# Cross attention of a decoder in groups of 4, 4, 4, 2 and 2 batches, and an expert layer with weights loaded a layer earlier and its sums in parts

## The reference

```python
# part 5: the weighted key-value recurrence of layer 1; reads ctx by channels only
# part 6: the experts of layer 1 (16 experts, 4 for each token, at most 128 tokens an expert)
scores = softmax(x @ gate_w.T)
topk_w, topk_i = top_k(scores, 4);  topk_w = topk_w / topk_w.sum(-1)
xg   = x[tokens of expert e]                                   # gathered rows
mid  = silu(xg @ w_gate[e]) * (xg @ w_up[e])                   # 176 wide
y[tokens of expert e] += (mid @ w_down[e]) * weight
shared = (silu(x @ sw_gate) * (x @ sw_up)) @ sw_down           # 352 wide
out  = y + shared
# part 8: the cross attention of layer 2, ctx as keys and values
Q      = x @ W_q.T
scores = coef * einsum('bsd,bnd->bsn', Q, ctx)                 # 128 x 128 for each batch
thr    = the 54th largest score of each row
att    = softmax(where(scores < thr, -inf, scores))
out    = einsum('bsn,bnd->bsd', att, ctx) @ W_o.T
```

## Time and profile before

| | us |
|---|---|
| three runs | 2928.51, 2930.05, 2932.92 (median 2930.05) |
| the profiled execution | 2934.89 |
| its span | 2933.1 |
| from the span's start: recurrence begins | 1411.1 |
| experts begin | 1517.7 |
| layer 2 attention begins | 1675.1 |
| cross attention begins | 2151.4 |
| layer 2 feed-forward begins | 2279.5 |

### The profile page before, as it was taken

How to read it: one execution, slowest core, us unless ns; L and a number is a source line. 1 busy time by engine, 2 the same in 40 slices (tenths; PEclk the granted TensorE clock), 3 DMA queues, 4 the chain that set the end, 5 groups by cost and what they waited for, 6 DMA issues and landing times. The chain is left out here.

```text
span 2933.1 us, 45191 instructions
## 1 busy us (share of the span) xinstructions
PE 2248.4 (77%) x18630; PEld 1725.2 (59%) x18679; DVE 1900.4 (65%) x3121; ACT 1283.9 (44%) x1627; POOL 353.7 (12%) x161
## 2 busy tenths in 40 slices
PE   7975278999999999997138789999953457877643
PEld 4654146777777767777124579999933224554422
DVE  5765677778887788875882434334437785773676
ACT  4642155666666666664422133333321343443144
POOL 0000012222232222320115000000000011000000
PEclk9987689999999999998569899999986679997867
DMA  3000121122121221222125400000000000000000
GB/s 131 1 1 12 23 64 49 54 75 55 49 54 56 73 55 50 53 60 72 61 82 146 166 23 0 0 0 0 0 8 1 30 0 24 2 1 15 1 29 29
DMA packets 159610, 117.72 MB, mean 40 GB/s; under 512 B 116176, under 2 KB 146000, under 8 KB 153680
## 3 DMA queue, kind: packets, MB, share of 16 engines
q1 hardware_dynamic: 156368, 110.99, 12.3%
q0 software_dynamic: 3072, 4.33, 0.9%
HBM read 97.64 MB, written 17.64 MB: 39 GB/s over the span
## 5 line engine op out<-in xcount | busy, mean ns | idle before, releaser
L1447 DVE SCALAR_TENSOR_TENSOR ctx_chan<-l1a_raw,l1a_cw,ctx_chan 128x1024 f32<-128x1024 f32 x192 | 230.8, 1275 | 19.5 <-ACT ctx_chan L1298 18.5
L1060 PE MATMUL banks<-x_chan,l1a_wp 128*128 128x512 f32 x512 | 230.6, 604 | 5.0 <-DMA l1a_wp<-in_l1a_wp_dram 5.0
L1024 POOL TENSOR_TENSOR l1a_sq<-ctx_chan 128x1024 f32<-128x1024 f32 x16 | 152.3, 9517 | 356.7 <-ACT ctx_chan L1302 356.7
L1060 PEld LDWEIGHTS banks<-x_chan,l1a_wp 128*128 128x128 f32 x512 | 98.1, 194 | 116.9 <-issue 110.8
L2475 PE MATMUL banks<-x_chan,l2a_wq 128*128 (+1 forms) x1024 | 124.2, 282 | 9.5 <-ACT l2a_ready L2378 4.9
L2475 PEld LDWEIGHTS banks<-x_chan,l2a_wq 128*128 128x128 f32 x1024 | 122.6, 198 | 11.4 <-issue 5.6
L1097 PE MATMUL banks<-l1a_wo,l1a_oT 128*128 128x256 f32 x512 | 121.8, 387 | 0.0
L1045 POOL TENSOR_TENSOR l1a_al<-l1a_aT,l1a_outer 128x1024 f32<-128x1024 f32 x32 | 74.8, 2359 | 327.2 <-DVE l1a_aT L1507 327.2
L2496 PE MATMUL banks<-l2a_wo,l2a_oT 128*128 128x256 f32 x512 | 113.2, 379 | 1.2 <-ACT l2a_oT L2402 1.2
L96 PE MATMUL banks<-ident,x_tok 128*128 128x128 f32 x288 | 56.8, 360 | 74.5 <-DVE x_tok L134 58.5
L1068 PE MATMUL banks<-l1a_wz,x_chan 128*128 128x256 f32 x512 | 113.7, 380 | 0.0
(11 more groups left out here) (604 smaller groups left out, 5908.2 us busy)
## 6 DMA issues: line engine op xcount, KB each, us to landing
ctx_tok<-l1a_rows_mem SPq DMA_DIRECT2D x16, 1024.0 KB, 6.6
l1a_sq<-l1a_norm_mem SPq DMA_DIRECT2D x16, 1024.0 KB, 4.5
ctx_tok<-in_ctx_dram SPq DMA_DIRECT2D x3, 2048.0 KB, 12.4
ctx_chan<-in_ctxT_dram SPq DMA_DIRECT2D x3, 2048.0 KB, 15.8
l1f_wgu<-in_l1f_wgu_dram SPq DMA_DIRECT2D x4, 1408.0 KB, 10.7
moe_sums<-l1x_zero SPq DMA_DIRECT2D x2, 2176.0 KB, 11.0
l1a_wp<-in_l1a_wp_dram SPq DMA_DIRECT2D x8, 512.0 KB, 3.3
l1f_wgu<-moe_sums SPq DMA_DIRECT2D x8, 512.0 KB, 8.1
```

What stands on the lines that cost most here:

```text
L1024: P.tensor_tensor(sq[:, 0, :], conv[:, 0, :], conv[:, 0, :], ALU.mult).then_inc(s["k_squared"], 1)
L1060: mm = MM(ps[:, 2 * (u % 2) + q, :], wp[:, c, u * 128:(u + 1) * 128], g.xT[:, c, t0:t0 + 512], start=c == 0, stop=c == 1)
L1447: V.scalar_tensor_tensor(t, raw[:, u, :, j:j + S], cw[:, c, j:j + 1], t, ALU.mult, ALU.add).then_inc(s["conv_done" if step == 2 else "conv ...
```

## The change

**Weights.** The last step of layer 1 attention no longer loads `ctx` into `g.mem`. The recurrence loads all of wd0 (2 MB, one transfer) there. The expert part then loads gate, up and wd1 of batches 0 and 1 at once, the routing weights behind them, and batches 2 and 3 once the eighth gather has landed.

**Experts.** `shared_in(3)`, its silu and its product are moved ahead of the experts. The sums are added quad by quad between the products of the shared chunks, and the normalising goes in parts of 8, 4 and 4 tiles.

**Cross attention.** The four quads of queries and scores follow each other, ACT moves and scales the scores, and DVE selects in groups of 4, 4, 4, 2, 2 batches. ACT takes the negated maximum as the exponential's bias. DVE makes mask, product and sum in one instruction for each batch, ACT divides before the transposes, PE adds x with a matmul by the identity, ACT moves the sum into x, and DVE takes the statistics of group n - 1 behind the selection of group n. Fourteen tiles are normalised while the last group is attended. wq and wo are laid out by partitions in DRAM.

```diff
@@ layer1_delta, SP
-            sp.dma_start(g.mem[:].rearrange("p b d -> p (b d)"), d["ctx"]).then_inc(s["restored"], 16)
             sp.dma_start(g.memT[:].rearrange("p c t -> p (c t)"), d["ctxT"]).then_inc(s["restored"], 16)
-            sp.wait_ge(s["restored"], 32)
+            sp.wait_ge(s["restored"], 16)
@@ layer1_wkv, SP
+            sp.dma_start(g.mem[:].rearrange("p b d -> p (b d)"), g.dram["l1f_wd0"]).then_inc(s["wd_loaded"], 16)
...
@@ layer1_moe, SP
             for n in range(4):
+                if n == 2:
+                    sp.wait_ge(fetched[RING - 1], 16)
                 sp.dma_start(wgu[:, e].rearrange("p e c h n -> p (e c h n)"), d["l1f_wgu"][n]).then_inc(w_loaded[n], 16)
-                sp.dma_start(wd0[:, e, :].rearrange("p e n -> p (e n)"), d["l1f_wd0"][n]).then_inc(w_loaded[n], 16)
                 sp.dma_start(wd1[:, e, :].rearrange("p e n -> p (e n)"), d["l1f_wd1"][n]).then_inc(w_loaded[n], 16)
-                if n == 0:
+                if n == 1:
                     sp.wait_ge(s["weights_made"], 1)
@@ layer1_moe, PE (ACT and DVE likewise: shared_silu(3), shared_mid(3))
             shared_in(2)
+            shared_in(3)
...
             def turn_mid(e):
+                if e == 0:
+                    pe.wait_ge(s["sh_mid"], 4)
...
-                for k in range(3):
-                    shared_in(3 * q + k)
+                for n in range(max(3 * q, 4), 3 * q + 3):
+                    shared_in(n)
@@ layer1_moe, DVE
-            for q in range(1, QUADS):
-                for k in range(3):
-                    shared_mid(3 * q + k)
-                if q < QUADS - 1:
-                    add_shared(q - 1)
-                if q == 2:
-                    v.wait_ge(s["sh_done"], 4)
-                    add_routed(0)
-                    add_routed(1)
+            shared_mid(4)
+            shared_mid(5)
+            add_shared(0)
+            v.wait_ge(s["sh_done"], 2)
+            shared_mid(6)
+            add_routed(0)
+            shared_mid(7)
+            shared_mid(8)
+            add_shared(1)
+            v.wait_ge(s["sh_done"], 4)
+            shared_mid(9)
+            add_routed(1)
+            shared_mid(10)
             add_routed(2)
-            add_shared(2)
+            shared_mid(11)
             add_routed(3)
             stats(0, 8, (s["chain"], count[0]))
-            stats(8, 12, (s["sh_done"], 6))
+            add_shared(2)
+            stats(8, EARLY, (s["sh_done"], 6))
             moments(0, EARLY)
+            normalise(0, 8, 1)
             add_shared(3)
...
@@ layer2_cross, PE, for each group (t0, t1) of GROUPS = ((0, 4), (4, 8), (8, 12), (12, 14), (14, 16))
+                pe.wait_ge(s["normed"], n + 1)
+                for i in range(t0, t1):
+                    mm = nc.tensor.transpose(ps[:, turned, (i - t0) * 128:(i - t0 + 1) * 128], probs[:, i, :], g.ident[:])
...
+                        nc.tensor.matmul(now, g.ident[:], g.x[:, i, :], start=True, stop=False)
+                        for c in range(DC):
+                            mm = nc.tensor.matmul(now, oT[:, i, c, :], wo[:, c, :], start=False, stop=c == 1)
@@ layer2_cross, ACT
+            for n in range(len(GROUPS)):
+                normed(n)
+                if n < len(GROUPS) - 1:
+                    exps(n + 1)
+                else:
+                    A(g.scratch[:], g.ones[:, 0:1], ACT.Sqrt)
+                    act.wait_ge(s["ln_var"], 1)
+                    A(g.rstd[:, 0:EARLY], g.rstd[:, 0:EARLY], ACT.Sqrt).then_inc(s["ln_sqrt"], 1)
+                attended(n)
@@ layer2_cross, DVE
+                v.wait_ge(s["exped"], n + 1)
+                for t in range(t0, t1):
...
+                    ins = V.scalar_tensor_tensor(probs[:, t, :], sc[:, t, :], best[:, t, at:at + 1], probs[:, t, :], ALU.is_ge, ALU.mult, accum_out=rsum[:, t:t + 1])
+                ins.then_inc(s["kept"], 1)
+                v.wait_ge(s["kept"], n + 1)
+                V.reciprocal(rsum[:, t0:t1], rsum[:, t0:t1]).then_inc(s["inverted"], 1)
...
+            for n in range(len(GROUPS)):
+                select(n)
+                if n:
+                    stats(*GROUPS[n - 1])
+                if n == len(GROUPS) - 1:
+                    moments(0, EARLY)
+                    normalise(0, EARLY, 1)
+            stats(*GROUPS[-1])
+            moments(EARLY, B)
+            normalise(EARLY, B, 2)
```

More of the change, by code:

```diff
@@ L2574, in _ @@
+            sp.dma_start(wo[:].rearrange("p c n -> p (c n)"), d["l2x_wo"]).then_inc(s["wo_loaded"], 16)
         @block.tensor
         def _(pe):
[L2576 to L2584 removed]
@@ L2604, in _ @@
[L2604 to L2612 removed]
+            pe.wait_ge(s["wq_loaded"], 16)
@@ L2613, in _ @@
+            pe.wait_ge(s["moved"], B // 2)
             pe_turn_x(pe, g, s["ln_out"], s["x_turned"], s["x_turned_out"])
@@ L2624, in _ @@
[L2624 to L2631 removed]
+            A = nc.scalar.activation
@@ new lines, in queries_moved, with scores_moved @@
+            def queries_moved(q):
+                for m in range(DC):
+                    act.wait_ge(s["queries"], q * DC + m + 1)
+                    A(qT[:, m, q * 512:(q + 1) * 512], ps[:, (q * DC + m) % 2, :], ACT.Copy).then_inc(s["q_out"], 1)
+            def scores_moved(q):
+                act.wait_ge(s["scores"], q + 1)
+                if q == 0:
+                    act.wait_ge(s["coef_made"], 1)
+                A(sc[:, q * GROUP:(q + 1) * GROUP, :].rearrange("p t n -> p (t n)"), ps[:, 2 + q % 2, :], ACT.Identity, scale=coef[:, 0:1]).then_inc(s["sc_out"], 1)
@@ new lines, in normalise @@
+            def normalise(t0, t1, part):
+                v.wait_ge(s["ln_sqrt"], part)
+                link(V.reciprocal(g.rstd[:, t0:t1], g.rstd[:, t0:t1]))
+                for t in range(t0, t1):
+                    V.tensor_scalar(g.x[:, t, :], g.x[:, t, :], g.moments[:, t, 0:1], g.rstd[:, t:t + 1],
+                                    ALU.subtract, ALU.mult).then_inc(s["ln_out"], 1)
+            for n in range(len(GROUPS)):
[5 more added lines that the diff above has]
+                    normalise(0, EARLY, 1)
```

208 lines of the change are left out of this document (114 added, 94 removed).

## The result

The changed kernel takes **2883.25 us** (median of 4 runs, 2877.60 to 2884.83) against 2930.44 (4 runs, 2928.51 to 2932.92): a ratio of 0.9835, 95% interval 0.9818 to 0.9852, thus 47.2 us less. Forecast were 2886 us, from 2876 to 2897.

A forecast was written before the change was run, and what follows sets the result against it. No engine is full and a barrier closes each part, so only shortening a part's chain counts. Experts -10.9 and cross attention -33.3 give -44.2 us: 2890.7 for the profiled execution, median 2886 us, range 2876 to 2897.

The forecast's parts named there:

- Experts, the start: Expert part: first gathered rows sooner and PE's clock kept up, so the experts end 5.2 us earlier.
- rival of slow gathers: Expert part: gathers take 8.3 us even with an empty queue, -2.9 becomes 0, total 2889 us; chance 0.05.
- Experts, the end: Behind the experts: PE ends at 1652.8, DVE at 1660.1 instead of 1671.0, turning and barrier 4.1 us as before.
- bold +2.3: End of the expert part: PE's last quad waits 2.3 us for `add_shared(2)`, which stands behind a sum and eight statistics.
- Cross attention, the head: Start of cross attention: DVE starts to select near 2164.5 against 2188.0, -23.5 us.
- Selection: DVE's selection in cross attention: 14.8 us for a group of 4, 8.3 for 2, 61.0 in all, +12.6 us.
- rival of free links: Cross attention selection: the links between DVE instructions cost nothing, total 2880 us; chance 0.05.
- The wait for group 2: Cross attention: group 2's chain of 13.7 us outlasts the selection of a group of 2, DVE waits +3.4 us.
- The tail: Cross attention behind the last reciprocal: 13.2 us where it was 43.2, -30.0 us.
- The first rival: Cross attention: PE stays at 1.2 GHz in the groups, waits and tail grow, total 2896 us; chance 0.12.
- Slower, serial groups: Cross attention: DVE waits for each group's whole chain, +67 us, so 22 us slower, 2953 us; chance 0.02.

The follow-up runs named there:

- eight_groups: Changed kernel with eight selection groups of 2 batches in place of 4, 4, 4, 2, 2: median 2905.8 us, cross attention 114.0 us.
- cross_alone: Kernel before with only the new cross attention and its host layout: median 2893.5 us, ratio 0.9902 to the kernel before.
- sized_fills: Changed kernel with small idle matmuls ahead of PE's waits, the root's table load and four expert-part copies moved earlier: median 2875.99 us, ratio 0.9829.
- exps_behind_copies: Changed kernel with ACT's exponentials of the next group behind a group's whole chain, not right behind its divisions: median 2888.4 us, cross attention 102.1.

## Why the prediction was right, and where a step was not

- *Experts, the start.* Forecast -5.2 us; the last expert's result comes 6.5 us earlier in the part (82.4 for 88.9), of which 0.6 lie ahead of the first gather. First landing 3.1 us (I had taken 2.8), no DMA wait, full clock: as forecast. **The step that failed is the cause**: I gave this gain to the hold on batches 2 and 3. Without the hold the part is as long; with wd0 back as well it is 3.2 longer. I had costed wd0's move at nothing, since I asked only whether the recurrence hides it, and not what its absence frees. By my own sum, a landing of 5.9 us without the hold puts the rows at 1554.4, with PE free at 1553.8: the chunk covers nearly all of it. In the rival of slow gathers I misread "the later ones took 4.1": that is the median of all 16 in the earlier trace rows, and the last eight took 2.8 to 2.9.
- *Experts, the end.* The stall of PE was forecast as 2.3 us and measured 2.17, but it was not on the path: DVE's own dense work sets that end. The sum of the prediction had this already without my seeing it, since it lets DVE go on from its own 1653.8 and not from PE's 1652.8; the bold +2.3 was no term of the -10.9. The turning behind DVE took 5.2 us for "4.1 us as before": PE had been idle for 3.8 us, since ACT held the copies behind its second root, and turned its 24 tiles at 0.23 us each, where the last 16 before took 0.15. From the last result to DVE's end it was 58.4 us, -6.0 for my -5.7. So -6.5 for -5.2 at the start, -6.0 for -5.7 and +1.1 for nothing: that the sum of -11.4 is so near to -10.9 is in part luck.
- *Cross attention, the head.* Selection begins 11.7 us into the part (forecast 13.1): -24.9 for -23.5. PE begins 2.8 us into the part, where it was 4.6. What the new layouts of wq and wo are worth in this was not run by itself.
- *Selection.* 14.7 and 8.3 us, forecast 14.8 and 8.3. The fixed 1.9 us of a group agree with 0.12 for a link, so the rival of free links is out. (For the rounds before, 7 x 3.2 + 6 x 4.3 is 48.2, not 48.4: without weight.) The Trainium skill (VectorE: DVE Perf Modes, The DRAIN you can't avoid) has a semaphore behind every instruction cost nothing over one behind the last; here DVE must also wait on its own semaphore between short instructions, and for that case eight_groups and the 14.73 us speak against it. No run left the links out.
- *The wait for group 2.* 2.1 us (0.31 and 1.83) for 3.4 (my own 13.7 less 8.3 and 1.4 would be 4.0); beside it 0.7 for the statistics of group 0 that I had not counted. The chain was 12.7 us from the reciprocal to the last copy's end, 1 less than forecast, and with the clock up 11.3 (2187.62 to 2198.87).
- *The tail.* 13.2 us, forecast 13.2. It depends on the clock: 11.5 in cross_alone, up to 14.4 elsewhere.
- *The first rival*, PE at 1.2 GHz in the groups, was half true: group 1's reading ran at full clock (2.05 us), most of group 0's (3.31), group 2's and parts of groups 3 and 4 did not. The Trainium skill (TensorE: Matmul & The Clock Gate, HAM oscillation) has bursts between waits each start cold; in eight_groups the reading was slow in six of eight groups. What it cost behind group 1 is at most the 2.5 to 5 us that sized_fills took back together with the table load, less than the rival's 10.
- *Slower, serial groups.* This did not happen, but exps_behind_copies and eight_groups show how near ACT's queue is to it.

Cross attention -35.4 for -33.3, experts -11.4 for -10.9: -46.8 for -44.2. The medians differ by 47.2, and unchanged parts scatter by more than the difference between these numbers.

## What to carry to other kernels

When a load is moved out of a stage, price what it leaves behind: the first small transfer of that stage no longer queues behind it, and a hold put in beside it may be worth nothing. A count of landings that leaves out the first transfers says nothing of them: take the time from the issue to the instruction that waited. When an engine's queue serves several chains, put first what the bottleneck engine will wait for next; that one order was worth 8 to 11 us here. A wait on one engine costs only if the engine that ends the stage is short of work because of it: look for the engine with no gap in the last microseconds.
